# A causal attention block whose fifth query tile per head is transposed on VectorE through a DRAM scratch

## What is computed

```python
xn = _layernorm(x)                                   # x: 1 x 1024 x 256
qkv = xn @ qkv_w + qkv_b                             # 16 heads of 128
scores = einsum('bhid,bhjd->bhij', q, k) + alibi     # -inf above the diagonal
attn = softmax(scores)
ctx = einsum('bhij,bhjd->bhid', attn, v)
out = x + (ctx @ out_w + out_b) + ghost_ffn(xn)      # FFN 256 -> 688 -> 256, weights = lut[idx]
```

## Time and profile before

| | |
|---|---|
| median of 3 runs | 524.1 us (523.46 to 524.34) |
| the profiled execution's own time | 524.43 us |
| its span in the profile | 522.6 us |
| granted TensorE clock | 1.0 of full |

### The profile page before, as it was taken

The page is one execution under the profiler, slowest core; times in us unless marked ns, Lnnn a source line. Parts: engine busy times, 40 slices in busy tenths (PEclk is TensorE's granted clock), DMA queues, the critical chain, the costliest instruction groups (busy, mean ns, idle before and its releaser), DMA issues.

```text
span 522.6 us, 10649 instructions
## 1 busy us (share of the span) xinstructions
PE 513.4 (98%) x3222; PEld 464.7 (89%) x3222; DVE 405.8 (78%) x1064; ACT 306.5 (59%) x657; POOL 336.8 (64%) x388
## 2 busy tenths in 40 slices
PE   8988999999999999999999999999999999999998
PEld 7777889989999889988998999988998899888897
DVE  7689787889778978978788977897897869864451
ACT  4777566656564746666665656474666556564430
POOL 3445867678667966586767866796658647872300
PEclk9999999999999999999999999999999999999999
DMA  7630100010000100000001000010000000000001
GB/s 272 124 81 1 41 22 20 3 36 25 4 16 20 40 0 20 8 33 20 20 0 37 23 2 19 20 40 0 20 0 0 21 1 1 1 2 1 1 21 61
DMA packets 8326, 14.08 MB, mean 27 GB/s; under 512 B 1008, under 2 KB 4080, under 8 KB 8176
## 3 DMA queue, kind: packets, MB, share of 16 engines
q1 hardware_dynamic: 7264, 12.75, 7.8%
q0 software_dynamic: 1040, 1.05, 1.6%
HBM read 12.75 MB, written 1.05 MB: 26 GB/s over the span
## 4 chain that ended last, share of the span: by engine, by line
PE 90%; DMA 3%; DVE 3%; ACT 2%; POOL 1%; issue 1%; DVEq 0%; ACTq 0%; SPq 0%
PE ps_u L400 17%; PE ps_u L402 17%; PE ps_u L401 17%; PE ps_t L519 12%; PE ps_s L402 8%; PE ps_s L401 8%; PE ps_s L400 8%; DMA qk_raw<-w_qk 2%; PE ps_t L402 1%; PE ps_t L401 1%; PE ps_t L400 1%; ACT work L665 1%; ACT p_t_hi L672 1%; DMA acc<-x 1%; DVE work L801 1%
## 5 line engine op out<-in xcount | busy, mean ns | idle before, releaser
L1032 POOL TENSOR_TENSOR w_ffn<-w_ffn,term 128x1088 f32<-128x1088 f32 x60 | 152.5, 2541 | 9.9 <-DVE term L871 9.9
L665 ACT ACTIVATE work<-work,neg_max 128x128 f32<-128x128 f32 (+7 forms) x128 | 98.8, 772 | 30.1 <-DVE neg_max L856 30.1
L672 ACT ACTIVATE p_t_hi<-ps_t 128x512 fp32r<-128x512 f32 (+1 forms) x192 | 86.1, 484 | 35.4 <-PE ps_t L519 34.0
L1010 POOL TENSOR_SCALAR work<-work,inv_sum 128x128 f32<-128x128 f32 (+7 forms) x128 | 106.3, 831 | 0.0
L884 DVE TENSOR_TENSOR p_t_lo<-ps_t,p_t_hi 128x512 fp32r<-128x512 f32 (+1 forms) x192 | 99.1, 544 | 9.2 <-ACT p_t_hi L672 8.6
L856 DVE CUSTOM_DVE_ANT_0 work<-ps_s,alibi 128x128 f32<-128x128 f32 (+7 forms) x128 | 96.1, 751 | 4.1 <-issue 4.1
L519 PE MATMUL ps_t<-ident,work 128*128 128x128 f32 x576 | 84.3, 273 | 3.8 <-POOL work L1010 2.4
L1009 POOL TENSOR_TENSOR pad<-entry 128x1 f32<-128x1 f32 x128 | 27.1, 211 | 92.2 <-DVE inv_sum L878 91.0
L519 PEld LDWEIGHTS ps_t<-ident,work 128*128 128x128 f32 x576 | 68.7, 140 | 11.3 <-POOL work L1010 3.3
L400 PE MATMUL ps_u<-p_t_hi,v_hi 128*128 128x512 f32 x192 | 69.5, 362 | 0.0
L400 PE MATMUL ps_s<-qk_hi 128*128 128x256 f32 (+2 forms) x192 | 67.0, 349 | 0.0
(11 more groups left out here) (125 smaller groups left out, 1161.3 us busy)
## 6 DMA issues: line engine op xcount, KB each, us to landing
qk_raw<-w_qk SPq DMA_DIRECT2D x16, 256.0 KB, 2.6
w_ffn<-idx SPq DMA_DIRECT2D x1, 2176.0 KB, 10.6
v_raw<-w_v SPq DMA_DIRECT2D x8, 256.0 KB, 2.5
o_raw<-w_o SPq DMA_DIRECT2D x8, 256.0 KB, 2.5
acc<-b_out POOLq DMA_DIRECT2D x1, 1024.0 KB, 18.2
out<-acc SPq DMA_DIRECT2D x8, 128.0 KB, 1.7
acc<-x SPq DMA_DIRECT2D x2, 256.0 KB, 3.0
acc<-x SPq DMA_DIRECT2D x1, 512.0 KB, 5.5
```

Source lines behind the costliest of these rows:

```text
L665: act.activation(slot(i), slot(i), ACT.Exp, bias=neg_max[:, col:col + 1], scale=-1.0, accum_out=row_sum[:, col:col + 1]).then_inc(exp_done, 1)
L672: act.activation(p_rows(0, i, g), ps_t[:, room, 0:len(turned(i, g)) * P].rearrange("p (j q) -> p j q", q=P), ACT.Copy).then_inc(p_hi, 1)
L1010: pool.tensor_scalar(slot(i % NT), slot(i % NT), inv_sum[:, col:col + 1], 1.0, ALU.mult, ALU.mult).then_inc(normed, 1)
L1032: pool.tensor_tensor(piece, piece, term[:, :], ALU.add).then_inc(term_added, 1)
```

## The change

Tile 4 of each head (`PLACED = 4`) leaves the path of PE. `GROUPS[4]` becomes 0, so `turn`, `p_hi_of` and `p_lo_of` do nothing for it. In step 7 (`BLOCKS_AT`) DVE transposes the 128x640 tile in blocks of 32x32 into `blocks`. SP stores it with four DMAs of 32 partitions each (80 KB, runs of 640 B) to a DRAM scratch and, once these have landed, loads it back with one DMA into `raw` (320 KB, 2560 B a partition), which puts the small blocks in their places. In step 2 of the next head ACT rounds `raw` to `p_t_hi` (`place_hi`) and DVE makes `p_t_lo` (`place_lo`); `_pv1-` waits for the latter. The widening goes, and with it the zeroing. `p_t` has another layout, in which the half rows fit into each other. Units, weight conversions, `look_up` terms, the POOL additions and the alibi multiplication come in other steps.

```diff
-QK_W_AT = 4
-V_W_AT = 2
+QK_W_AT = 6
+V_W_AT = 4
 O_W_AT = 6
-ALIBI_AT = 3
-SUM_AT = 1
+ALIBI_AT = 2
+SUM_AT = 1, 2, 4, 7
+BLOCKS_AT = 7
+PLACED_HI_AT = 2
+PLACED_LO_AT = 2
+PLACED = 4
-GROUPS = [-(-(i + 1) // 4) for i in range(NT)]
+GROUPS = [-(-(i + 1) // 4) if i != PLACED else 0 for i in range(NT)]
 def pt_from(half, j):
-    return min(max(0, j - 4 * half) * P, 2 * P)
+    return max(0, j - 4 * half) * P
     STEADY: [
-        (("q1", 0), ("_out0", 0), ("k1", 1), ("_out1", 1), ("nq0", 2), ("_pv1-", 3), ("_pv1", 4),
-         ("v0", 5), ("v1", 6), ("nk0", 6), ("pv0", 7), ("v2", 7)),
-        (("k1", 0), ("q1", 0), ("v3", 1), ("_out2", 1), ("_out3", 2), ("_pv1-", 4), ("_pv1", 4),
-         ("nk0", 6), ("nq0", 6), ("pv0", 7)),
+        (("k1", 0), ("_out0", 0), ("q1", 1), ("nq0", 2), ("_out1", 2), ("_pv1-", 4), ("_pv1", 4),
+         ("nk0", 4), ("v0", 5), ("v1", 5), ("v2", 6), ("pv0", 7)),
+        (("_out2", 0), ("q1", 0), ("k1", 1), ("v3", 2), ("_out3", 2), ("_pv1-", 4), ("_pv1", 4),
+         ("nq0", 6), ("nk0", 6), ("pv0", 7)),
...
-TAIL = (("turn", 5), ("gate_up", 0), ("out", 0), ("out", 1), ("turn", 6), ("gate_up", 1), ("turn", 7),
+TAIL = (("turn", 5), ("placed", PLACED), ("gate_up", 0), ("out", 0), ("out", 1), ("turn", 6), ("gate_up", 1), ("turn", 7),
...
+            def move(n, p):
+                sp.wait_ge(blocks_turned, head_no(n, p) + 1)
+                for a in range(BANDS):
+                    sp.dma_start(scratch[:, :, a, :].rearrange("b p x -> p b x"),
+                                 blocks[a * B32:(a + 1) * B32, :, :, :].rearrange("p b j c -> p b (j c)")
+                                 ).then_inc(blocks_out, 16)
+                sp.wait_ge(blocks_out, n * (32 * BANDS) + (p + 1) * (16 * BANDS))
+                sp.dma_start(raw[:, :], scratch[:, :, :, :].rearrange("b p a x -> (b p) (a x)")).then_inc(blocks_back, 16)
...
                 sp.dma_start(qk_raw[:, :, :], w_qk[n * 2 + 3]).then_inc(qk_landed, 16)
+                move(n, 0)
...
+                    if c == 1:
+                        pe.wait_ge(placed_lo, head_no(n, p))
...
-                wide = max(per, 2 * P)
                 for b in range(banks):
-                    last = three(ps_s[:, i % 2, b * HALF:b * HALF + wide],
+                    last = three(ps_s[:, i % 2, b * HALF:b * HALF + per],
...
+            def place_hi(n, p):
+                act.wait_ge(blocks_back, n * 32 + p * 16 + 16)
+                act.activation(placed_rows(0), placed_raw(), ACT.Copy).then_inc(placed_hi, 1)
...
+            def turn_blocks(n, p):
+                dve.wait_ge(normed, tile_no(n, p, PLACED) + 1)
+                if not (isinstance(n, int) and n == 0 and p == 0):
+                    dve.wait_ge(blocks_out, n * (32 * BANDS) + p * (16 * BANDS))
+                dve.transpose(blocks[:, :, :, :].rearrange("p b j c -> p j b c"),
+                              slot(PLACED).rearrange("p (j b c) -> p j b c", b=BANDS, c=B32)).then_inc(blocks_turned, 1)
+            def place_lo(n, p):
+                dve.wait_ge(placed_hi, head_no(n, p) + 1)
+                dve.tensor_tensor(placed_rows(1), placed_raw(), placed_rows(0).bitcast(F32),
+                                  ALU.subtract).then_inc(placed_lo, 1)
```

More of the change, by code:

```diff
@@ L60 @@
 SLOT_AT = [sum(SLOT_W[:i]) for i in range(4)]
[L64 to L67, removed]
+PT_ROW = HALF
+PT_BACK = HALF + P
+PT_COLS = (NT + 1) * PT_ROW
 REST = INTER - (FT - 1) * P
@@ L120 @@
         ("gate_up", 11))
+TERM_FIRST_AT = 4, 5, 6, 7
+TERM_SECOND_AT = 1, 3, 4, 7
+TERM_AT = 1, 2, 4, 7
+TERM_LATE_AT = 1, 3, 5, 7
 def term_at(kind, p, i):
[L125 to L128, removed]
+    if kind == FIRST:
+        at = TERM_SECOND_AT if p else TERM_FIRST_AT
+    else:
+        at = TERM_LATE_AT if (kind, p) == (LAST, 0) else TERM_AT
+    return at.index(i) if i in at else None
 def units_of(kind, p, begun=False):
@@ L180, in block_ffn @@
         work = sb("work", [P, sum(SLOT_W)])
+        raw = sb("raw", [P, BANDS * BAND])
+        blocks = sb("blocks", [P, BANDS, PLACED + 1, B32])
         xn_t = [sb(f"xn_t_{s}", [P, KT, S], F32R) for s in ("hi", "lo")]
@@ L252, in turned, with placed_raw, placed_rows, head_no @@
         def turned(i, g):
-            return range(4 * g, min(4 * g + 4, i + 1))
+            return range(4 * g, min(4 * g + 4, i + 1)) if i >= 4 else range(i, -1, -1)
         def p_rows(part, i, g):
[L258 to L265, removed]
+            js, q = turned(i, g), (i % 4) * P
+            if i >= 4:
+                at = pt_at(1, js[0]) + q
+                rows = p_t[part][:, at:at + len(js) * PT_ROW].rearrange("p (j q) -> p j q", q=PT_ROW)
+                return rows[:, :, 0:P]
+            end = pt_at(0, 0) + q + P
+            rows = p_t[part][:, end - len(js) * PT_BACK:end].rearrange("p (j q) -> p j q", q=PT_BACK)
+            return rows[:, :, PT_BACK - P:]
+        def placed_raw():
+            return raw[:, :].rearrange("p (a j c) -> p j a c", a=BANDS, c=B32)
+        def placed_rows(part):
+            rows = p_t[part][:, 0:(PLACED + 1) * PT_ROW].rearrange("p (j q) -> p j q", q=PT_ROW)
+            return rows[:, :, 0:P].rearrange("p j (a c) -> p j a c", c=B32)
+        def head_no(n, p):
+            return 2 * n + p
         def tile_no(n, p, i):
@@ L585, in _ @@
                     gate_up(no)
+                elif what == "placed":
+                    continue
                 elif what == "pv":
                     pe.wait_ge(p_lo, HEADS * HEAD_GROUPS)
+                    pe.wait_ge(placed_lo, HEADS)
                     units += 1
@@ L687, in pair @@
                             p_hi_of(n, p, t, i < LAG)
+                        if i == PLACED_HI_AT and not (kind == FIRST and p == 0):
+                            place_hi(n, p - 1)
                         for name, step in units_of(kind, p):
@@ L743, in _ @@
                     p_hi_of(PAIRS, 0, no, True)
+                elif what == "placed":
+                    place_hi(PAIRS - 1, 1)
                 elif what == "gate_up":
@@ L809, in xn_lo_of @@
                                       ALU.subtract).then_inc(xn_lo, 1)
-            zero0, zero1 = pt_at(0, 3) + 2 * P, pt_at(1, 7) + 2 * P
-            for part in range(2):
-                dve.memset(p_t[part][:, zero0:zero0 + P].bitcast(F32), 0.0)
-                last = dve.memset(p_t[part][:, zero1:zero1 + P].bitcast(F32), 0.0)
-            last.then_inc(cleared, 1)
             statistics(0)
@@ L849, in mask @@
                     dve.wait_ge(alibi_ready, 2 * n + p + 1)
-                if not (kind == FIRST and p == 0 and i < 4):
+                if i == 0 and not (kind == FIRST and p == 0):
+                    dve.wait_ge(blocks_turned, head_no(n, p))
+                elif i >= 4 or not (kind == FIRST and p == 0):
                     dve.wait_ge(p_turned, groups_to(n, p, i - 4))
@@ L904, in pair @@
                             p_lo_of(n, p, t, i < LAG)
+                        if i == PLACED_LO_AT and not (kind == FIRST and p == 0):
+                            place_lo(n, p - 1)
+                        if i == BLOCKS_AT:
+                            turn_blocks(n, p)
                         if i == NT - 1:
@@ L951, in _ @@
                     p_lo_of(PAIRS, 0, no, True)
+                elif what == "placed":
+                    place_lo(PAIRS - 1, 1)
                 elif what == "gate_up":
@@ L1025, in pair @@
                                                ALU.subtract).then_inc(o_w_lo, 1)
-                        if not (kind == FIRST and p == 0) and i % 2 == SUM_AT:
-                            part = i // 2
+                        if not (kind == FIRST and p == 0) and i in SUM_AT:
+                            part = SUM_AT.index(i)
                             pool.wait_ge(term_ready, n * (2 * TERMS) + p * TERMS + part + 1)
```

26 lines of the change are left out of this document (19 added, 7 removed), and 7 rows, old and new, of the table UNITS.

## The result

| | before | changed |
|---|---|---|
| median | 523.83 us (6 runs, 523.30 to 524.34) | 525.50 us (6 runs, 524.69 to 526.27) |
| ratio | 1 | 1.0031, 95% interval 1.0017 to 1.0046 |
| profiled execution, its span | 524.43, 522.6 us | 524.69, 522.9 us |
| a steady pair of heads | 56.61 us | 56.66 us |
| start of mask 0 of head 1 / of the last head | 40.5 / 436.5 us | 38.9 / 436.1 us |

515.1 us had been predicted. (A pair is measured from mask 0 of one head to mask 0 two heads on, as the mean of the six pairs of the loop, heads 2 to 13. The start of head 1 and the tail are one sample each.) One of the five executions of experiment 3 took 2840.55 us at full clock and stays out of every comparison here.

What follows compares the result with a forecast made beforehand. PE's stream of matmuls was taken to bound the kernel. Transpositions -8.6, narrow matmuls -1.4 and waits +1.0 gave -9.0; 524.43 - 9.0 - 0.3 (profiled execution to median) = 515.1 us, range 508 to 522.

Steps and rivals of the forecast that it cites:

- That lies beside PE's work and costs nothing by itself: DVE's extra 0.66 us a head, with `place_lo` at 0.81 us, was to run beside PE's matmuls at no cost.
- What moved: Moved units and later data: 0.5 us charged for the tail, 0.5 us for short waits in the loop.
- Transpositions, -8.6 us: Step 7, between scores and context: removing five PE transpositions saves 0.54 us in each of 16 heads.
- Narrow matmuls, -1.4 us: Tile 0 scores and context units' last block row: 144 matmuls at 128 columns, not 256, save 0.01 us each.
- rival 1: Weight loads don't set the floor for narrow matmuls, saving 6.5 us more: 508.6 us, chance 0.10.
- rival 3: Narrow float32r matmuls run at a quarter of the rate, +15.8 instead of -1.4: 532.3 us, chance 0.11.
- DVE's 48.3 us a pair: DVE's work in a steady pair of heads after the change, 87% busy instead of 83%.
- The 32x32 transposition at 0.8 us: DVE's transposition of tile 4 in step 7, taken at the mask's price of 0.8 us.
- Trip of 6.5 us, hidden: Tile 4's stores to DRAM and load back take 6.5 us, hidden in 11 us of room before `place_hi`.
- rival 4: The DRAM trip is late and ACT waits before `place_hi`; a trip of 13 us gives 525.6, chance 0.04.
- Rival 2: DVE and ACT become late; PE waiting 0.3 us a head gives back 4.8 us: 519.9 us, chance 0.14.
- Steady pair of 55.3 us with PE busy all through: Sign of a right forecast: two heads in the loop take 55.3 us, against 56.60, without PE waits.

Runs made afterwards that it cites:

- experiment 3: The changed kernel without `place_lo`, tile 4's lo part zeroed once and missing from the result, PE's matmuls the same: 517.46 us.
- experiment 1: The kernel before with only the narrow matmuls added, 128 columns where 128 are needed: 521.86 us.
- experiment 5: The changed kernel with tile 4 transposed by PE again; narrow matmuls, new `p_t` layout and new steps kept, last head's `_pv1` one step earlier: 526.94 us.
- experiment 10: The changed kernel with the steps of before, `_pv1-` one step later and no `place_lo`, tile 4's lo part staying zero: 513.98 us.
- experiment 7: The changed kernel with the steps of before, but `_pv1-` of a pair's first head in step 4, not 3: 516.31 us.
- experiment 9: The kernel before with the narrow matmuls and `_pv1-` one step later, tile 4 still transposed by PE: 521.74 us.
- experiment 11: The changed kernel with `place_lo` one step later in DVE's order, step 3 instead of 2: 600.04 us.
- experiment 6: The changed kernel with the first table look-up of a head one step earlier on DVE, step 0 instead of 1: 535.29 us.

## Why the prediction was wrong

**Two steps of the prediction failed, and they failed together.** One is the sentence on `place_lo`, "That lies beside PE's work and costs nothing by itself". Its 0.81 us is right for the instruction alone (816 ns), but in the new steps it takes 1.73, holds up POOL for another 0.6, and its presence costs 8.0 us (experiment 3). The other is "What moved", with its charge of 0.5 us for short waits in the loop and 0.5 in the tail: experiments 1 and 5 give the new steps alone 5.1 us. Four kernels that differ in just these two things show how they join:

| | without `place_lo` | with it |
|---|---|---|
| steps of before, one unit later | 513.98 us (experiment 10) | 516.31 us (experiment 7) |
| new steps | 517.46 us (experiment 3) | 525.50 us (changed kernel) |

`place_lo` by itself costs 2.3 us and the new steps by themselves 3.5. Together they cost 11.5, so 5.7 us come only where both are: the new steps put POOL's addition of 2.5 us right beside `place_lo`. What in the new steps costs the 3.5 stays open.

Point by point:

- *Transpositions, -8.6 us.* Right in a steady pair: 1.16 us (experiments 9, 7), and 16 x 0.58 would be 9.3. Of this 5.4 us reach the time in experiment 7. The six pairs of the loop give 6.9 and head 1 0.4, but the head before the last is 0.8 longer, with its long `place_lo`, and so is the tail (86.9 us from the last head's start against 86.1). That all 16 heads have the transpositions in the full stream was too much said.
- *Narrow matmuls, -1.4 us.* Right: 1.9 measured, pitch 0.11. Rivals 1 and 3 are out: 0.06 appears only at the first matmul of a unit's last row, a quarter of the rate nowhere.
- *DVE's 48.3 us a pair.* Right in experiment 7, 48.43. In the changed kernel 48.71 is right by luck, a long `place_lo` against shorter look-ups. And it was the wrong question: what decides is beside which POOL instruction each piece lies.
- *The 32x32 transposition at 0.8 us.* Right: 825 ns. The Trainium skill's 311 ns for a 128x128 block in bf16 ("VectorE: DVE Perf Modes", The three transpose paths), 1.56 us for five by estimate, is not what this trace shows for float32.
- *Trip of 6.5 us, hidden.* Hidden, with one wait of 0.6 us, in the tail (6.3 us there), so rival 4 is out. But in the loop the trip took about 7.4 us and the room was 8.2, not 11: it was nearer than the chance of 0.04 says.
- *Rival 2, DVE and ACT late, 519.9 us.* Right in kind: PE's new waits are for DVE and for POOL behind DVE. It was priced at 0.3 us a head; the steady pair shows 0.7 (56.66 - 55.27 = 1.4 a pair), which in the six pairs of the loop is 8.4 us of the miss of 10.4. ACT wasn't late. It had a chance of 0.14.
- *Steady pair of 55.3 us with PE busy all through.* 56.66 with waits. Experiment 7 shows 55.27.

The forecast treated POOL as a bystander. The earlier trace rows have it busy for 41.02 of 56.60 us, half of it with the additions (8 x 2.54), so that an instruction placed at random on DVE and sensitive to it meets one more often than not.

## What to carry to other kernels

When work moves from one engine to another, look where its operands lie: a DVE subtraction with one input in PSUM (`p_t_lo` of before) and one with both in SBUF (`place_lo`) cost about the same per column alone, and only the second stops for POOL's addition and then stops POOL. Look in the order of both engines for what will run beside it. Here look-ups, with one input tensor in SBUF, met POOL's work too. And measure the new path with the old order first: here the order ate the gain, and undoing it with one context unit a step later gave -1.5% instead of +0.3%. Where an engine is fully busy, one late operand in front of it costs its whole wait in every round, so the unit that reads the new result is the first thing to move.

## What the runs showed of the hardware

- Two SBUF inputs on DVE against POOL's addition: 816 ns alone, 1.73 us with the wait, 2.22 in experiment 11; POOL's one-column operation behind it 0.78 us instead of 0.20.
- One input in PSUM instead (`p_t_lo`, 512 columns) beside the same addition: at most 0.693 us, 0.68 alone. A look-up, one input tensor in SBUF, beside POOL's scaling: 1.67 us, 0.84 alone (experiment 6).
- The 32x32 transposition of 128x640 float32: 825 ns, as much as the mask of that width, 816.
- A pause of 3.93 us on PE in the midst of full work was followed by 3.4 us at 1.2 GHz, one of 3.65 by 6.8 us (experiment 11). The waits of up to 1.7 us in experiment 6 left the clock at 1.00. But in the first head of experiment 10's profiled execution a pause of 1.89 us, up to 36.10, was followed by 3.4 us at 1.2 GHz too.
- A 128-column float32r matmul starts 0.11 us behind the one before, as a 256-column one does 0.12, and 0.06 only behind the first one of the context unit's last row.
